# Layer 0 of a two-layer graph network: one gather per chunk of edges, and node sums kept with channels on partitions

## The reference

```python
h = relu(layernorm(x))
# layer 0, per channel: a softmax over the edges of each destination node
a  = (h @ W_src.T + b_src)[src] + (h @ W_dst.T + b_dst)[dst]
e  = where(a >= 0, a, 0.2 * a)
ex = exp(e - segment_max(e, dst)[dst])
x  = x + segment_sum((h @ W_v.T + b_v)[src] * ex / segment_sum(ex, dst)[dst], dst)
h = relu(layernorm(x))
# layer 1: two small MLPs on the edge features and on gathered node rows give a message and eight
# attention logits per edge; a softmax over all edges; sums by destination; a product; a layernorm
x = x + layer1(h)
```

## Time and profile before

| stage, us | PE busy | DVE busy | ACT busy | POOL busy | clock |
|---|---|---|---|---|---|
| prepare, 0 to 170 | 55.6 | 105.6 | 85.4 | 12.8 | 0.90 |
| layer0_edges, 170 to 1532 | 991.6 | 1308.3 | 773.0 | 1016.6 | 0.98 |
| node_tables, 1532 to 1672 | 53.7 | 102.6 | 67.4 | 31.4 | 0.73 |
| layer 1 and the end, 1672 to 3500 | 1690.9 | 1011.5 | 1115.5 | 1024.7 | 0.97 |

### The profile page before, as it was taken

The page is one execution under the profiler, slowest core; times in us unless marked ns, Lnnn a source line. Parts: engine busy times, 40 slices in busy tenths (PEclk is TensorE's granted clock), DMA queues, the critical chain, the costliest instruction groups (busy, mean ns, idle before and its releaser), DMA issues. The chain is left out here.

```text
span 3499.8 us, 76247 instructions
## 1 busy us (share of the span) xinstructions
PE 2791.7 (80%) x17156; PEld 1977.5 (57%) x17380; DVE 2528.0 (72%) x4445; ACT 2041.3 (58%) x4527; POOL 2085.4 (60%) x2160
## 2 busy tenths in 40 slices
PE   1577777777777777744799999999999999958885
PEld 0355555555555555532466666666666666647774
DVE  5699999999999999996345555555554555567776
ACT  6355555555555555545355555555555555568885
POOL 0177777777777777732777777777777777500001
PEclk9899999999999999978899999999999999989997
DMA  2555444554444444413777777777777777647662
GB/s 71 172 143 145 142 142 141 142 144 144 142 139 141 143 141 143 141 34 106 206 218 222 218 218 221 220 218 221 217 222 220 220 220 218 190 132 202 202 202 82
DMA packets 391734, 595.68 MB, mean 170 GB/s; under 512 B 73317, under 2 KB 237855, under 8 KB 391682
## 3 DMA queue, kind: packets, MB, share of 16 engines
q0 software_dynamic: 98304, 268.57, 27.1%
q1 hardware_dynamic: 242626, 247.55, 25.4%
q10 hardware_dynamic: 50752, 78.99, 6.6%
HBM read 501.15 MB, written 93.68 MB: 170 GB/s over the span
## 5 line engine op out<-in xcount | busy, mean ns | idle before, releaser
L1194 POOL DMA_INDIRECT l_G<-rows_d,l_sidx x1024 | 1002.5, 979 | 363.1 <-issue 276.3
L807 POOL DMA_INDIRECT l_G<-rows_d,l_sidx x1024 | 1014.0, 990 | 330.5 <-issue 305.0
L1322 ACT ACTIVATE l_h<-l_H,l_cols 128x512 f32<-128x512 f32 x512 | 350.7, 685 | 557.3 <-PE l_H L1229 540.5
L875 PE MATMUL l_accp<-l_we,l_ohe 128*128 128x256 f32 x2048 | 486.3, 380 | 0.0
L831 PE MATMUL l_A<-ident,l_G 128*128 128x128 f32 x1024 | 172.8, 293 | 380.6 <-DVE l_oht L978 323.0
L1386 DVE TENSOR_TENSOR big<-l_SC,l_b 128x512 f32<-128x512 f32 x256 | 177.1, 692 | 387.9 <-PE l_SC L1258 387.9
L875 PEld LDWEIGHTS l_accp<-l_we,l_ohe 128*128 128x128 f32 x2048 | 371.1, 191 | 40.1
L831 PEld LDWEIGHTS l_A<-ident,l_G 128*128 128x128 f32 x1024 | 111.2, 144 | 482.0 <-issue 243.5
L1258 PEld LDWEIGHTS l_SC<-big,l_h 128*128 128x128 f32 x2048 | 263.6, 191 | 146.8 <-issue 146.8
L1548 PE MATMUL ag_accp<-ag_msg,ag_pick 128*128 128x128 f32 x2048 | 286.5, 288 | 73.7 <-ACT ag_msg L1532 32.9
L903 ACT ACTIVATE l_qe<-l_A 128x512 f32<-128x512 f32 x256 | 153.3, 599 | 325.8 <-PE l_A L834 209.7
(11 more groups left out here) (182 smaller groups left out, 5755.4 us busy)
## 6 DMA issues: line engine op xcount, KB each, us to landing
msg_d<-l_msg ACTq DMA_DIRECT2D x256, 256.0 KB, 2.2
ag_msg<-msg_d SPq DMA_DIRECT2D x256, 256.0 KB, 2.9
l_G<-rows_d,l_sidx POOLq DMA_INDIRECT x2048, 3.3
l_lo<-mark_d SPq DMA_DIRECT2D x256, 128.0 KB, 3.0
l_lo<-code_d SPq DMA_DIRECT2D x256, 128.0 KB
l_in<-in_ea_dram SPq DMA_DIRECT2D x512, 64.0 KB
l_fd<-dst_d SPq DMA_DIRECT2D x256, 96.0 KB, 3.4
l_pd<-dst_d SPq DMA_DIRECT2D x256, 96.0 KB
```

The source lines that it names most:

```text
L807: nc.gpsimd.indirect_dma_start(out=G[:, s, j, :], out_offset=None, in_=rows_d[0][:, :], in_offset=bass.IndirectOffsetOnAxis(ap=sidx[:, hal ...
L875: last = nc.tensor.matmul(accp[b][:, 0:2 * C], oh_e[:, b, j, :], we_t[:, b, j, :], start=(j == 0), stop=(j == TJ - 1), skip_group_check=True)
L1194: nc.gpsimd.indirect_dma_start(out=G[:, s, j, :], out_offset=None, in_=rows_d[1][:, :], in_offset=bass.IndirectOffsetOnAxis(ap=sidx[:, hal ...
L1322: nc.scalar.activation(out_t[:, s % 2, :], in_p[:, :], ACT.Silu, bias=cols[:, col:col + 1]).then_inc(ready, 1)
```

## The change

Layer 0 gathers each chunk once, into the slot chunk mod 8 of the same ring. POOL counts chunks that have landed (`here`); before it fills a slot again it reads from a table how many items come before the end of the chunk that was in it (`passed_row`) and waits for that many weighted products. A new ACT pass (`fetch`) copies an item's source terms out of its chunk's slot, found by a register, and PE's front half reads that copy. DVE's product reads the slot by a register too.

The sums now have channels on partitions: `collect` takes weights and weighted values as stationary operands and the one-hot as the moving one. The chunk's first factor then belongs to one column of the sums, that of the node of the chunk's first edge (`first_row`; a spare column where there is none to scale), and DVE multiplies 128 x 2 values by it. The spread column, the mask and the pass over the block go. `prepare` makes the new tables, and `node_tables` turns the quotient by PE before DVE adds it to X.

```diff
 POOL, layer 0
-                        def gather(lap, u, d):
-                            i, v, lp = item(lap, u, d, 2 * U)
...
-                            if after(i, U):
-                                hold(pool, pool_passed, (wv_ready, i - U + 1))
...
+                        def gather(lap, u):
+                            c, v, lp = item(lap, u, 0, 2 * U)
                             s, half = v % U, v // U
+                            if exists(c, CHUNKS):
+                                if after(c, U):
+                                    done = pool.value_load(passed_row[0:1, bass.ds(c - U, 1)], min_val=1, max_val=NI)
+                                    hold(pool, pool_passed, (wv_ready, done))
...
+                                for j in range(TJ):
+                                    nc.gpsimd.indirect_dma_start(
+                                        out=G[:, s, j, :], out_offset=None, in_=rows_d[0][:, :],
...
+                            c, v, lp = item(lap, u, -1, 2 * U)
+                            if exists(c, CHUNKS):
+                                hold(pool, pool_passed, (gat[v % U], 16 * TJ * (2 * lp + v // U + 1)))
+                                pool.sem_inc(here, 1)
 PE, layer 0
-                            pe.wait_ge(gat[s], 16 * TJ * (lp + 1))
+                            pe.wait_ge(fetched, i + 1)
...
-                                nc.tensor.matmul(av[:, j, :], G[:, s, j, 0:C], ident[:, :], is_transpose=True,
+                                nc.tensor.matmul(av[:, j, :], fs_t[:, b, j, :], ident[:, :], is_transpose=True,
...
-                            nc.tensor.matmul(accp[b][:, 2 * C:3 * C], w_t[:, g, 0:1].to_broadcast([P, P]), ident[:, :],
-                                             is_transpose=True, start=True, stop=True, skip_group_check=True)
-                            for j in range(TJ):
-                                last = nc.tensor.matmul(accp[b][:, 0:2 * C], oh_e[:, b, j, :], we_t[:, b, j, :],
-                                                        start=(j == 0), stop=(j == TJ - 1), skip_group_check=True)
+                            for k in range(2):
+                                for j in range(TJ):
+                                    last = nc.tensor.matmul(accp[b][:, k, :], we_t[:, b, j, k * C:(k + 1) * C], oh_e[:, b, j, :],
+                                                            start=(j == 0), stop=(j == TJ - 1))
 ACT, layer 0
+                        def fetch(lap, u, d):
+                            i, s, lp = item(lap, u, d)
+                            if not exists(i, NI):
+                                return
+                            at = act.value_load(items_row[0:1, bass.ds(i * FIELDS + 2, 1)], min_val=0, max_val=(U - 1) * SLOT)
+                            count = act.value_load(items_row[0:1, bass.ds(i * FIELDS, 1)], min_val=1, max_val=CHUNKS)
+                            act.wait_ge(here, count)
+                            if after(i, 2):
+                                act.wait_ge(a_ready, i - 1)
+                            nc.scalar.activation(fs_t[:, s % 2, :, :],
+                                                 G_all[:, bass.ds(at, SLOT)].rearrange("p (j r) -> p j r", j=TJ)[:, :, 0:C],
+                                                 ACT.Copy).then_inc(fetched, 1)
...
-                            nc.scalar.activation(rest_of[:, g:g + 1], oht[:, g, 0:1], ACT.Copy, scale=-1.0,
-                                                 bias=1.0).then_inc(rest_ready, 1)
...
                             link(lap, u, 1)
+                            fetch(lap, u, 3)
                             whose(lap, u, 4)
 DVE, layer 0
-                            dve.wait_ge(gat[s], 16 * TJ * (lp + 1))
+                            at = dve.value_load(items_row[0:1, bass.ds(i * FIELDS + 2, 1)], min_val=0, max_val=(U - 1) * SLOT)
...
-                            nc.vector.tensor_tensor(we_t[:, b, :, C:2 * C], we_t[:, b, :, 0:C], G[:, s, :, C:2 * C],
+                            nc.vector.tensor_tensor(we_t[:, b, :, C:2 * C], we_t[:, b, :, 0:C],
+                                                    G_all[:, bass.ds(at, SLOT)].rearrange("p (j r) -> p j r", j=TJ)[:, :, C:2 * C],
                                                     ALU.mult).then_inc(wv_ready, 1)
...
-                            dve.wait_ge(accp_ready, i + 1)
...
-                            nc.vector.scalar_tensor_tensor(out=mine,
-                                                           in0=accp[b][:, 2 * C:3 * C].unsqueeze(1).to_broadcast([P, 2, C]),
-                                                           scalar=rest_of[:, g:g + 1], in1=mine,
-                                                           op0=ALU.max, op1=ALU.mult).then_inc(acc_scaled, 1)
...
+                            at = dve.value_load(first_row[0:1, bass.ds(i, 1)], min_val=0, max_val=OTHER)
+                            mine = acc0[:, :, bass.ds(at, 1)]
+                            dve.wait_ge(w_ready, i + 1)
...
+                            nc.vector.tensor_scalar(mine, mine, w_t[:, g, 0:1], None, ALU.mult).then_inc(acc_scaled, 1)
...
+                            at = dve.value_load(items_row[0:1, bass.ds(i * FIELDS + 1, 1)], min_val=0, max_val=NB * P)
+                            mine = acc0[:, :, bass.ds(at, P)]
+                            dve.wait_ge(accp_ready, i + 1)
...
+                            nc.vector.tensor_tensor(mine, mine, accp[s % 2][:, :, :], ALU.add).then_inc(acc_done, 1)
 node_tables: POOL, PE, DVE
-                            if q < GROUPS:
-                                pool.wait_ge(s_quotient, q + 1)
-                                nc.gpsimd.tensor_tensor(X[:, span(q), :], X[:, span(q), :], w[:, span(q), :],
-                                                        ALU.add).then_inc(s_sum, 1)
...
+                        for q in range(GROUPS + 2):
+                            back(q, 0)
+                            back(q, 1)
+                            if q >= 2:
+                                pe.wait_ge(s_h, GB * (q - 1))
+                                turn(pe, (q - 2) * PAIRS)
+                            for g in pairs(q - 2):
+                                if g + 1 in pairs(q - 2):
                                     turn(pe, g + 1)
                                 product(pe, g)
+                            back(q, 2)
...
+                                for k, part in enumerate(PARTS):
+                                    n = (q - 1) * len(PARTS) + k
+                                    mine = X[:, (q - 1) * GB + part[0]:(q - 1) * GB + part[-1] + 1, :]
+                                    dve.wait_ge(s_turned, n + 1)
+                                    nc.vector.tensor_tensor(mine, mine, quo[n % 2][:, 0:len(part), :], ALU.add).then_inc(s_sum, 1)
```

More of the change, by code:

```diff
@@ L393, in prepare @@
                 pick = sb("pr_pick", [P, 8], F32, st)
-                table = sb("pr_table", [P, 2, 2], I32, st)
+                table = sb("pr_table", [P, 2, FIELDS], I32, st)
+                slot_i = sb("pr_slot", [P, 2], I32, st)
+                below = sb("pr_below", [P, NI], F32, st)
+                passed = sb("pr_passed", [P, 2], F32, st)
+                passed_i = sb("pr_passed_i", [P, 2], I32, st)
                 base = sb("pr_base", [P, 2], F32, st)
@@ L599, in _ @@
                             low(dve, g - 2)
+                            if g == SOURCES_AT:
+                                dve.wait_ge(s_chosen, 2 * TJ)
+                                for h in range(TJ // 2):
+                                    mine = src_tab.rearrange("p (c j) -> p j c", j=TJ)[:, 2 * h:2 * h + 2, :]
+                                    nc.vector.tensor_copy(mine, chosen[h][:, :, 0:CHUNKS]).then_inc(s_took, 1)
                             if g == CHOICE_AT:
@@ L609, in _ @@
                                 nc.vector.tensor_copy(mine_bc[:, :], mine_i[:, :].bitcast(F32))
+                                for q in range(2):
+                                    link(nc.vector.tensor_scalar(below[:, :], chunk_bc[:, :], iota_col[:, q:q + 1], None,
+                                                                 ALU.is_le))
+                                    link(nc.vector.tensor_reduce(passed[:, q:q + 1], below[:, :], AX_X, ALU.add))
+                                nc.vector.tensor_copy(passed_i[:, :], passed[:, :]).then_inc(s_passed, 1)
                             if g == FIRST_AT:
-                                dve.wait_ge(s_chosen, 2 * TJ)
+                                dve.wait_ge(s_chosen, 4 * TJ)
                                 for h in range(TJ // 2):
@@ L668, in _, with back @@
                         pe.wait_ge(s_in, 16)
[L669 to L673, removed]
+                        def back(q, k):
+                            if not 0 <= q < GROUPS:
+                                return
+                            n = q * len(PARTS) + k
+                            if k == 0:
```

(12 more changed lines are left out.)

140 lines of the change are left out of this document (88 added, 52 removed).

## The result

The changed kernel takes 3517.48 us (median of 5 runs, 3514.44 to 3527.22) beside 3502.27 for the kernel before in the same runs: 1.005 of it, 95% interval 1.0036 to 1.0065. It is slower by some 15 us, clear of the interval; 3427, faster, was forecast, and the range ended at 3485.

A forecast was written before the change was run, and what follows sets the result against it. POOL's gathers set the edge loop's pace, with DVE 4% behind. Loop -95.6, start of ring and loop turns +2, preparation +4, node stage +15: -75 us, 3427 us at the median; range 3389 to 3485.

The forecast's parts named there:

- Gathers: Layer 0's edge loop: 1024 gathers become 832, still 1.326 us each, so POOL needs 1103 us, 5.30 per chunk.
- POOL leaves the path: Edge loop: POOL needs 5.30 us per chunk where DVE uses one up in 6.04, so POOL no longer sets the pace.
- DVE's step: Edge loop: the shorter scaling takes DVE's time per item from 5.09 to 4.91 us, leaky ReLU to scan 0.82.
- New waits on POOL's queue: Edge loop: register load (0.7 us), slot wait and landing wait per chunk have cover; uncovered load makes 6.00 us per chunk.
- POOL bound again: Rival, chance 0.11: POOL's queue drains once per chunk in the edge loop, 6.80 us per chunk, 3580 us in all.
- point of decision: Edge loop: from 6.41 us per chunk, 5.21 per item, the loop's gain no longer pays for the other stages.
- PE, ACT and the loads of DVE: Edge loop: PE's at worst 0.4 us more, ACT's fetch of 0.63 us and DVE's two new register loads are hidden.
- Node stage: Stage after the edge loop: turning the quotient on PE and adding it on DVE cost +15 us together.
- PE's order: Node stage: PE waits for a group's quotient before starting products of the group two back; taken as +10 us.
- the adds: Node stage: DVE's adds of some 1.7 us replace POOL's 2.88 us add; +5 us over three groups.
- the node stage gains: Rival, chance 0.08: only the ratio of the two adds counts, -6 us in place of +15, 3406 us in all.
- Preparation: Before the edge loop: DVE's new copies, count and small steps, some 6 us, partly hidden by waits for PE; +4 us.

The follow-up runs named there:

- run 1: Changed kernel with DVE's sum put between leaky ReLU and first scan, and the next item's scaling between the scans; 3430.41 us, 0.9799 of the kernel before.
- run 4: Changed kernel with POOL's register load and wait for the ring slot done twice per chunk; 3518.18 us.
- Run 8: run 1's kernel, with PE making a group's products first and turning the new quotient after the third; 3414.86 us, 0.9749 of the kernel before.
- run 7: Changed kernel with one more small DVE product per item before the first scan, scaling on a fixed column without its register load; 3528.36 us.

## Why the prediction was wrong, step by step

- **Gathers, the step that failed:** "At the present 1.326 us each, index copies included, POOL needs 1103 us". From the first start to the last, 832 gathers took 1339 us, 1.612 each, 6.45 us per chunk. I took a duration from the kernel before and let it stand while I moved the operations of DVE that it depends on; the conclusion "POOL leaves the path" fell with it. The rows had the sign: gathers of 947 ns at the median and 1841 at most, one of 1.43, and a DVE step on ten elements stretched to 2.37 us beside POOL's add. It ended at 1560.97, 0.02 us behind that add (1558.07 + 2.88), and I read it as a curiosity of that stage.
- **DVE's step:** right. 4.89 for 4.91, and 0.79 from leaky ReLU to scan for 0.82. Once POOL keeps up, the loop has about the gain predicted: run 1's scans give 255 x (4.89 - 5.285) = -101 for -95.6.
- **New waits on POOL's queue:** right. They have cover (run 4, and pauses of 0.30 us between the gathers). The rival "POOL bound again" named the right engine and about the right point of decision (6.41 us per chunk, by its own figures rather 6.40; 6.45 came), by a mechanism that did not occur: the queue did not drain. That the time landed so near this point is chance.
- **PE, ACT and the loads of DVE:** right so far as the loop shows it: in run 1 all of them lie inside 4.89 us.
- **Node stage:** right in place, and in size partly by luck, +16.0 for +15. The prediction names no row for its 4.6 us of new work on PE ahead of a group's first product; DVE waits 4.85 to 5.89 us for that product in three groups, where the kernel before had no wait (the first of the three is the eviction at 1573.04):

```profile
1568.55 1.49 DVE L795 TENSOR_TENSOR big<-big 128x1280 f32<-128x1280 f32 x1
1574.89 0.96 DVE L305 COPY n_row<-n_pp 128x768 f32<-128x768 f32 x1 [4.85 <-PE n_pp L284]
...
1604.25 0.96 DVE L305 COPY n_row<-n_pp 128x768 f32<-128x768 f32 x1 [5.89 <-PE n_pp L284]
...
1632.91 0.96 DVE L305 COPY n_row<-n_pp 128x768 f32<-128x768 f32 x1 [4.86 <-PE n_pp L284]
```

  Run 8 gives these back by PE's order alone: the stretch from first reciprocal to first gather is 155.3 us in run 1, 140.1 in run 8 and 139.8 before. So PE's order accounts for some 15 us where +10 was taken, which leaves next to nothing for the adds, where +5 was taken: the sum came out right because the two errors cancelled. The rival in which the node stage gains is not borne out, as even run 8's is no shorter than before.
- **Preparation:** too small, +12.1 for +6 with the start. DVE's new steps add 6.2 us to its busy time up to the first scan (106.84 to 113.01), for the 6 taken, but they do not disappear into its waits for PE (17.9 before): these grow by 2.4, and the time for which the trace shows no cause by 2.6 (5.8 before). What DVE waits for between 60 and 170 us after the change:

```profile
DVE n_row L307 <- PE n_pp L284: 20.3, 9, 4.9
...
DVE n_row L307 <- issue: 8.4, 2, 4.9
```

  No experiment was made on this part.

## What to carry to other kernels

The duration of a gather that POOL issues is a property of the schedule beside it and not of the instruction: before such a duration goes into a sum, lay POOL's and DVE's order of time on each other and see in which DVE operation each gather begins. When two engines run in a fixed pattern, count how many operations of one fit in a step of the other, before and after; a step made 0.2 us shorter can lose a whole one. Another order of the same operations can then be worth more than a shorter operation (87 us in run 1).

## What the runs showed of the hardware beyond that

A loop turn of DVE that is a little longer can cost much more than its instructions. One product and its wait more for each of eight items raised the instruction packets from 41 to 186 and the time by 117 us over run 7, some 3.7 us per turn of the loop. Run 7 has the product too but fewer register instructions. The Trainium skill says in "Runtime: NRT & Kernel Launch", Instruction fetch mechanics, that a branch to code outside the two blocks held at the time makes the engine fetch it first; the packets agree, and where the limit lies no run here shows.
